# One transformer block on one core: the self-attention stage with its softmax reciprocal on GpSimd, its rotation in two products, its statistics woven and one power for two layer norms

## The reference, cut to what matters

```python
x = x + xattn(layernorm(x), ctx_1024, ...)            # cross-attention, its own layer norm behind it
x = x + attn(layernorm(x), ...)                       # self-attention: the stage that is changed
x = x + ffn(layernorm(x), ...)                        # a shared expert and 2 of 8 routed ones

def attn(x):                                          # x: 64 sequences of 64 rows, 256 columns
    q, k, v = (x @ W.T + b  per W, b), split in 16 heads of 16 columns
    q, k = rope(q), rope(k)                           # x1*cos - x2*sin ; x1*sin + x2*cos on the two halves of a head
    scores = q @ k.T * 16**-0.5
    attn = softmax(scores, axis=-1)
    return (attn @ v) @ Wo.T + bo
layernorm(x) = (x - mean) / sqrt(var + 1e-5)
```

## Time and profile before

| what | value |
| --- | --- |
| time, median of 3 runs | 2171.07 us (2169.53 to 2171.08) |
| time of the profiled execution | 2171.83 us |
| its span | 2170.1 us |
| TensorE busy, share of the span | 2109.5 us, 97% |
| VectorE busy | 1576.1 us, 73% |
| ScalarE busy | 1275.5 us, 59% |
| GpSimd busy | 951.1 us, 44% |
| softmax product of tile 0 starts (L1430) | 1409.33 us |
| softmax product of tile 31 starts | 1644.40 us |

### The profile page before, as it was taken

The page is one execution under the profiler, slowest core; times in us unless marked ns, Lnnn a source line. Parts: engine busy times, 40 slices in busy tenths (PEclk is TensorE's granted clock), DMA queues, the critical chain, the costliest instruction groups (busy, mean ns, idle before and its releaser), DMA issues.

```text
span 2170.1 us, 46318 instructions
## 1 busy us (share of the span) xinstructions
PE 2109.5 (97%) x15864; PEld 1851.0 (85%) x15865; DVE 1576.1 (73%) x2833; ACT 1275.5 (59%) x3067; POOL 951.1 (44%) x813
## 2 busy tenths in 40 slices
PE   8999999999999999999999999899998999999997
PEld 7898888898888888888888888677776888888886
DVE  7667767767767677677677676689996887666665
ACT  5566666656656665666656556477775335555553
POOL 5223322322333332233223323388885234777775
PEclk9999999999999999999999999999999999999999
DMA  4000000010010010000100100245533222333332
GB/s 154 11 21 25 22 22 24 10 34 19 14 34 19 14 34 14 19 24 13 31 24 10 34 10 1 81 140 152 152 121 100 88 78 54 54 53 53 54 55 42
DMA packets 100686, 103.91 MB, mean 48 GB/s; under 512 B 11952, under 2 KB 90160, under 8 KB 100624
## 3 DMA queue, kind: packets, MB, share of 16 engines
q1 hardware_dynamic: 86992, 84.47, 12.6%
q0 software_dynamic: 13632, 18.62, 5.3%
HBM read 72.52 MB, written 30.54 MB: 47 GB/s over the span
## 4 chain that ended last, share of the span: by engine, by line
PE 59%; DVE 17%; issue 9%; POOL 9%; ACT 3%; DMA 2%; DVEq 0%; POOLq 0%; SPq 0%; ACTq 0%
PE banks L915 33%; PE banks L958 6%; PE banks L988 5%; PE banks L1016 5%; POOL out_dram L2393 4%; PE banks L1003 3%; POOL r_x L2357 3%; DVE top L678 2%; DVE q_st L658 2%; DMA out_dram<-r_y,index 2%; PE banks L2232 2%; POOL index L2364 2%; DVE peak L675 2%; DVE s_peak L1550 1%; DVE s_rsum L1596 1%
## 5 line engine op out<-in xcount | busy, mean ns | idle before, releaser
L915 PE MATMUL banks<-ctxT_hi,qk_hi 128*128 128x256 f32 x1024 | 300.8, 294 | 0.0
L915 PE MATMUL banks<-ctxT_hi,qk_lo 128*128 128x256 f32 x1024 | 289.8, 283 | 0.0
L915 PE MATMUL banks<-ctxT_lo,qk_hi 128*128 128x256 f32 x1024 | 287.4, 281 | 0.0
L547 ACT ACTIVATE probs<-banks,nbias 128x256 f32<-128x256 f32 x512 | 236.0, 484 | 83.7 <-DVE nbias L680 83.3
L436 POOL TENSOR_TENSOR rinv<-rsum,inverse 128x4 f32<-128x4 f32 x96 | 96.7, 1008 | 408.3 <-ACT probs L547 408.3
L554 ACT ACTIVATE pc<-banks 128x512 f32<-128x512 f32 x256 | 153.0, 598 | 191.0 <-PE banks L915 187.9
L638 DVE TENSOR_TENSOR qk_lo<-banks,qk_hi 128x512 fp32r<-128x512 f32 x256 | 163.4, 685 | 88.0 <-ACT qk_hi L509 88.0
L675 DVE TENSOR_REDUCE peak<-banks 128x4 f32<-128x1024 f32 x128 | 156.3, 1221 | 90.6 <-PE banks L915 90.4
L915 PE MATMUL banks<-pT_hi,ctx_hi 128*128 128x512 f32 x512 | 205.2, 401 | 1.7 <-DVE pT_lo L638 1.7
L638 DVE TENSOR_TENSOR pT_lo<-banks,pT_hi 128x512 fp32r<-128x512 f32 x256 | 165.5, 684 | 56.7 <-ACT pT_hi L509 56.2
L915 PE MATMUL banks<-pT_hi,ctx_lo 128*128 128x512 f32 x512 | 202.3, 395 | 0.0
(11 more groups left out here) (273 smaller groups left out, 6195.1 us busy)
## 6 DMA issues: line engine op xcount, KB each, us to landing
ctx_raw<-in_ctx_dram SPq DMA_DIRECT2D x64, 256.0 KB, 2.7
experts_w<-in_L_ffn_We_dram SPq DMA_DIRECT2D x24, 512.0 KB, 4.0
x_in<-in_x_dram SPq DMA_DIRECT2D x16, 256.0 KB, 2.8
x_again<-in_x_dram SPq DMA_DIRECT2D x16, 256.0 KB, 2.8
x_stream<-z SPq DMA_DIRECT2D x16, 256.0 KB, 2.1
s_x<-x_stream SPq DMA_DIRECT2D x32, 128.0 KB, 3.8
s_x_again<-x_stream SPq DMA_DIRECT2D x32, 128.0 KB, 2.1
x_normalised<-s_xl SPq DMA_DIRECT2D x32, 128.0 KB, 1.7
```

What stands on the lines that cost most here:

```text
L547: nc.scalar.activation(probs[:, s % 2, p, :], scores[:, s % 2, p // 2, (p % 2) * SK:(p % 2 + 1) * SK], ACT.Exp, bias=nbias[:, s % 2, p:p + ...
L915: last = nc.tensor.matmul(out, a, b, start=(n == 0), stop=(n == 3 * len(pairs) - 1))
```

## The change

Four edits, all in the self-attention stage:

1. VectorE's RECIPROCAL of the 16 softmax sums is gone. GpSimd raises the sums to the power -1 (a `tensor_tensor` with 128x16 elements) right before the softmax product, with a wait on `rsum_done` ahead of it and a wait for its own result behind it.
2. The rotation's three products become two of 512 columns, over a table in another order, into one tile `spun` with two halves; GpSimd adds the halves as it did before.
3. VectorE's statistics of the two layer norms stand together: two `bn_stats`, two `bn_aggr`, and one addition of epsilon on two columns. They stand ahead of the rotation; before, those of tile n-2 stood behind it.
4. GpSimd takes both inverse roots with one power on two columns at the head of the step; the second `rstd` power ahead of `xl` is gone.

```diff
-LINKS_PER_PAIR = 16
+LINKS_PER_PAIR = 12
...
-    table = np.concatenate([cos, cos, -sin, sin], axis=1)
+    table = np.concatenate([cos, sin, -sin, cos], axis=1)
...
-                sp.wait_ge(l3_stats, g.tile(s, -1))
+                sp.wait_ge(ln_stats, g.tile(s, 4))
...
-    def rotate(src, out_cos, out_sin, done):
+    def rotate(src, w):
...
-        done[0](nc.vector.tensor_tensor(heads(out_cos), heads(src), angles(0, HD), ALU.mult))
-        done[1](nc.vector.tensor_tensor(heads(out_sin)[:, :, 0:h], heads(src)[:, :, h:HD], angles(HD, h), ALU.mult))
-        done[2](nc.vector.tensor_tensor(heads(out_sin)[:, :, h:HD], heads(src)[:, :, 0:h], angles(HD + h, h), ALU.mult))
+        return nc.vector.tensor_tensor(
+            spun[:, w, :].rearrange("p (h e d) -> p h e d", e=2, d=h),
+            src.rearrange("p (h w d) -> p w h d", w=2, d=h)[:, w].unsqueeze(2).broadcast_to([P, 2 * SH, 2, h]),
+            table[:, w * HD:(w + 1) * HD].rearrange("p (e d) -> p e d", d=h).unsqueeze(1).broadcast_to([P, 2 * SH, 2, h]),
+            ALU.mult)
...
-    def normalised(pool, out, src, which, ready, done, nth):
-        pool.wait_ge(ready, nth)
-        nc.gpsimd.tensor_tensor(rstd[:, which:which + 1], mv[:, which, 1:2], power[:, :],
-                                ALU.pow).then_inc(done, 1)
-        pool.wait_ge(done, nth)
-        pool.sem_inc(pool_past, 1)
+    def inverse_spread(pool, g, s):
+        first, second = g.has(s, 3), g.has(s, -2)
+        if first or second:
+            pool.wait_ge(ln_stats, g.tile(s, 4))
+            which = slice(0 if first else 1, 2 if second else 1)
+            nc.gpsimd.tensor_tensor(rstd[:, which], mv[:, which, 1], power[:, which], ALU.pow).then_inc(rstd_done, 1)
+            pool.wait_ge(rstd_done, g.tile(s, 4))
+            pool.sem_inc(pool_past, 1)
...
     def pool_step_at(pool, g, s):
+        inverse_spread(pool, g, s)
...
-            nc.gpsimd.tensor_tensor(turned[:, :], turned[:, :], swapped[:, :], ALU.add).then_inc(turn_done, 1)
+            nc.gpsimd.tensor_tensor(turned, turned, spun[:, 1, :], ALU.add).then_inc(turn_done, 1)
...
         if g.has(s, 0):
+            pool.wait_ge(rsum_done, g.tile(s, 1))
+            nc.gpsimd.tensor_tensor(rinv[:, :], rsum[:, :], inverse[:, :], ALU.pow).then_inc(rinv_done, 1)
             pool.wait_ge(rinv_done, g.tile(s, 1))
...
-            ln_of(dve, x1[:, o, :], 0, ln_stats)
+            stats_1 = stats_of(x1[:, o, :], 0)
+        if g.has(s, -2):
+            wait_freed(dve, g, ("y", s))
+            stats_2 = stats_of(x2[:, s, :], 1)
+        if g.has(s, 3):
+            means = mean_of(dve, 0, stats_1)
+        if g.has(s, -2):
+            if g.has(s, -3):
+
+                dve.wait_ge(l3_done, g.tile(s, -2))
+            means = mean_of(dve, 1, stats_2)
+        if g.has(s, 3) or g.has(s, -2):
+            dve.wait_ge(dve_step, means)
+            which = slice(0 if g.has(s, 3) else 1, 2 if g.has(s, -2) else 1)
+            nc.vector.tensor_scalar(mv[:, which, 1], mv[:, which, 1], EPS, None, ALU.add).then_inc(ln_stats, 1)
...
-            link(nc.vector.tensor_reduce(rsum[:, :], probs[:, s, :].rearrange("p (h k) -> p h k", k=SQ),
-                                         AX_X, ALU.add))
-            nc.vector.reciprocal(rinv[:, :], rsum[:, :]).then_inc(rinv_done, 1)
+            nc.vector.tensor_reduce(rsum[:, :], probs[:, s, :].rearrange("p (h k) -> p h k", k=SQ),
+                                    AX_X, ALU.add).then_inc(rsum_done, 1)
```

More of the change, by code:

```diff
@@ L1219, in self_attention @@
     bvp = sb("bvp", [P, DC])
-    power = sb("power", [P, 1])
+    inverse = sb("inverse", [P, SH])
+    power = sb("power", [P, 2])
     x1 = sb("x1", [P, 2, D])
@@ L1228, in self_attention @@
     xT_lo = sb("xT_lo", [P, 2, DC, P], F32R)
-    turned = sb("turned", [P, 2 * D])
-    swapped = sb("swapped", [P, 2 * D])
+    spun = sb("spun", [P, 2, 2 * D])
+    turned = spun[:, 0, :]
     qT = sb("qT", [P, DC, P])
@@ L1255, in self_attention @@
     ln_stats = sem("ln_stats")
-    ln_rstd = sem("ln_rstd")
+    rstd_done = sem("rstd_done")
     ln_done = sem("ln_done")
-    l3_stats = sem("l3_stats")
-    l3_rstd = sem("l3_rstd")
     l3_done = sem("l3_done")
@@ L1396, in pool_start, with normalised @@
         nc.gpsimd.memset(share[:, :], 2.0 / P).then_inc(pool_setup, 1)
+        nc.gpsimd.memset(inverse[:, :], -1.0).then_inc(pool_setup, 1)
         nc.gpsimd.memset(vbd[:, :, :, :, :, :], 0.0).then_inc(pool_setup, 1)
-        pool.wait_ge(pool_setup, 3)
-    def normalised(pool, out, src, which, ready, done, nth):
-        pool.wait_ge(ready, nth)
-        nc.gpsimd.tensor_tensor(rstd[:, which:which + 1], mv[:, which, 1:2], power[:, :],
-                                ALU.pow).then_inc(done, 1)
-        pool.wait_ge(done, nth)
-        pool.sem_inc(pool_past, 1)
+        pool.wait_ge(pool_setup, 4)
+    def inverse_spread(pool, g, s):
[6 more added lines that the diff above has]
+            pool.sem_inc(pool_past, 1)
+    def normalised(out, src, which):
         return nc.gpsimd.tensor_scalar(out, src, mv[:, which, 0:1], rstd[:, which:which + 1],
@@ L1414, in pool_step_at @@
             o = (s + 1) % 2
-            normalised(pool, xn[:, :], x1[:, o, :], 0, ln_stats, ln_rstd, g.tile(s, 4)).then_inc(ln_done, 1)
+            pool.sem_inc(pool_past, 1)
+            normalised(xn[:, :], x1[:, o, :], 0).then_inc(ln_done, 1)
         if g.has(s, 2):
             wait_freed(pool, g, ("qk", s))
-            nc.gpsimd.tensor_tensor(turned[:, :], turned[:, :], swapped[:, :], ALU.add).then_inc(turn_done, 1)
+            nc.gpsimd.tensor_tensor(turned, turned, spun[:, 1, :], ALU.add).then_inc(turn_done, 1)
         if g.has(s, -2):
@@ L1425, in pool_step_at @@
                 wait_filled(pool, g, key, pairs_on)
-            normalised(pool, xl[:, s, :], x2[:, s, :], 1, l3_stats, l3_rstd, g.tile(s, -1)).then_inc(l3_done, 1)
+            pool.sem_inc(pool_past, 1)
+            normalised(xl[:, s, :], x2[:, s, :], 1).then_inc(l3_done, 1)
         if g.has(s, 0):
+            pool.wait_ge(rsum_done, g.tile(s, 1))
+            nc.gpsimd.tensor_tensor(rinv[:, :], rsum[:, :], inverse[:, :], ALU.pow).then_inc(rinv_done, 1)
             pool.wait_ge(rinv_done, g.tile(s, 1))
@@ L1537, in dve_start, with stats_of, mean_of @@
         dve.wait_ge(bias_done, 1)
-    def ln_of(dve, src, which, ready):
-        link(nc.vector.bn_stats(stats[:, which, :], src))
+    def stats_of(src, which):
+        step(nc.vector.bn_stats(stats[:, which, :], src))
+        return chain[0] + chain[1]
+    def mean_of(dve, which, stats_at):
+        dve.wait_ge(dve_step, stats_at)
         dve.sem_inc(dve_past, 1)
-        link(nc.vector.bn_aggr(mv[:, which, :], stats[:, which, :]))
-        nc.vector.tensor_scalar(mv[:, which, 1:2], mv[:, which, 1:2], EPS, None, ALU.add).then_inc(ready, 1)
+        step(nc.vector.bn_aggr(mv[:, which, :], stats[:, which, :]))
+        return chain[0] + chain[1]
     def dve_step_at(dve, g, s):
@@ L1583, in dve_step_at @@
                 dve.wait_ge(turn_done, g.tile(s, 2))
[L1584 to L1587, removed]
-                dve.wait_ge(l3_done, g.tile(s, -2))
-            ln_of(dve, x2[:, s, :], 1, l3_stats)
+            step(rotate(bank, 0))
+            rotate(bank, 1).then_inc(free, 1)
         if g.has(s, 0):
@@ L1661, in pe_step @@
             for c in range(4):
-                last = nc.tensor.transpose(bank[:, c * P:(c + 1) * P], turned[:, c * P:(c + 1) * P], ident[:, :])
+                last = nc.tensor.transpose(bank[:, c * P:(c + 1) * P], spun[:, 0, c * P:(c + 1) * P], ident[:, :])
             last.then_inc(done, 1)
```

9 lines of the change are left out of this document (3 added, 6 removed).

## The result

The changed kernel takes 2233.28 us (median of 4 runs, 2232.52 to 2234.50), the kernel before 2171.07 us (median of 4, 2169.53 to 2173.85): a ratio of 1.0282 with a 95% interval of 1.0270 to 1.0295, 62 us slower. The prediction was 2225 us with a range of 2214 to 2244. The profiled execution took 2233.07 us, its span is 2230.9 us.

What follows compares the result with a forecast made beforehand. GpSimd was to become the bound at 9.45 us a step instead of 7.74. Middle +44.5, ramp +4.2 and tail +4.5 made +53.2 us on the profiled 2171.83: 2225 us, range 2214 to 2244.

Steps and rivals of the forecast that it cites:

- The power of 16 columns: GpSimd's new reciprocal: 2.82 us on a straight line through one, two and four columns, 3.03 us added with its gap.
- the steeper: Rival: the 16-column power costs 4.03 us, in proportion to four columns, giving 2264 us; chance 0.07.
- the flat: Rival: the power costs the same for 4 as for 16 columns, giving 2170 us, no change; chance 0.03.
- the cheap rival: Rival: the 16-column power costs 0.216 us like a plain product, TensorE becomes the bound, 2163 us; chance 0.04.
- One power for both norms: On GpSimd, two one-column powers with gaps, 1.54 us, become one two-column power, 0.91 us with its gap; 0.63 us saved.
- the sum for the middle: Tiles 2 to 28: 26 GpSimd steps of 9.45 us, 245.7 us where there were 201.2, +44.5 us.
- what comes behind the last product "stays": Tail behind the softmax product of tile 31: holds neither sums nor reciprocals, so its time was to stay unchanged.
- its first rival: Rival: gaps in every middle step lower TensorE's clock; at half the time lower, +14 us, 2239 us; chance 0.08.
- Which engine stands behind: Before the change, VectorE sets the step of 7.74 us and TensorE stands right behind at about 7.3 to 7.5 us.
- VectorE's savings land in a wait: In the middle, VectorE gains a wait of 2 to 3 us a step ahead of the sums or the maximum.
- The statistics: On VectorE, statistics waits get covered and one addition goes; with the reciprocal, 0.4 to 0.8 us off its step.
- TensorE's wait at L1714 and its loop: TensorE waits for GpSimd's softmax product 1.5 to 2.2 us a step; no loop but GpSimd's own is binding.

Runs made afterwards that it cites:

- no_inc: The changed kernel without one semaphore increment in GpSimd's queue behind the wait for the power of the two variances: 2231.40 us, ratio 1.0273.
- dve_recip: The changed kernel with the reciprocal of the softmax sums back on VectorE, the other three edits kept: 2169.64 us, ratio 0.9991 to the kernel before.
- fill: The changed kernel with 12 extra identity transposes on TensorE ahead of its wait for the softmax product in each of the 24 looped steps: 2233.98 us.
- pow8: The changed kernel with GpSimd's reciprocal power on 8 of the 16 columns, the other reciprocals a constant: 2194.82 us, ratio 1.0102 to the kernel before.
- pow8_split: The changed kernel with the reciprocal power on 8 columns and epsilon added in two one-column instructions instead of one of two columns: 2190.71 us.

## Why the prediction was right, point by point

The mechanism was the one forecast: GpSimd's own row sets the step, and its new power makes it. The profiled execution took 2233.07 us where 2225.0 was the sum, 8 us more. By the rows these are 4.2 in the middle, 2.0 behind the last product, 1.0 in the ramp, and about 1 in the next stage and around the span.

**The power of 16 columns: right.** Three rows on a line gave 2.82 us; it takes 2.923. With its gap (0.07, taken as 0.21) the term is 2.99 us where 3.03 stood: it was near by luck in part, since an error of 0.10 and one of 0.14 the other way cancel. The 2.923 us lie between both bounds, 1.01 and 4.03, and refute the steeper, the flat and the cheap rival; 1.661 us at 8 columns refutes a price by blocks.

**One power for both norms: the size of one term was off.** The power itself is 0.696 us (0.698 was read). The gap behind it is 0.31 to 0.38 us and not 0.21, because more stands in the queue between the power and its reader: 0.16 us a step, of which no_inc shows 0.08 and the rest is argued. This is most of what the sum for the middle lacked: 9.61 less 9.45 is 0.16, 4.2 us in 26 steps. The rest is small and goes both ways: the rotation's sum to `xl` 1.26 and not 1.23, the product to the power 1.86 to 2.01 and not 1.90. By the latter the products stand 9.55 to 9.73 us apart, where 9.4 to 9.5 without alternation was forecast.

**The step of the sum that failed: what comes behind the last product "stays".** It grew by 2.0 us, because the tail's TensorE now waits for GpSimd (2.46 us ahead of the L1714 of the last tile but one) and then runs at the lower clock, 0.50, up to the next stage; at 1.00 the stretch takes 11.06 us. The prediction had this mechanism as its first rival, but for the middle, where it costs nothing, and not for the tail, where each product and transpose is on the path. The ramp grew by 5.2 us where 4.2 stood; that 1 us is less than what executions differ by ahead of the stage.

**Which engine stands behind: right in name, wrong in size.** TensorE was said to stand at 7.3 to 7.5 us a step. It stands at 7.6. The 0.47 us that the earlier trace rows show at L1667 are idle time of weight loads, and 8.9 of their 12.2 us are still there in dve_recip, where TensorE is the bound. The real room was 0.15 us. It did not touch the forecast, since GpSimd's loop is far above both; but it made the expectation for dve_recip wrong, 2163 instead of 2169.6. The price of the cheap-power rival is too low by that.

**VectorE's savings land in a wait: right.** 2.6 us a step where 2 to 3 were forecast. The forecast had it ahead of the sums or of the maximum; two thirds of it stand ahead of `xT_lo` instead. The rotation in two products measures 1.27 to 1.29 us together, 0.67 to 0.69 each with an overlap: no gain and no loss against three, as taken.

**The statistics: counted as a gain, and partly a cost.** One addition less is right for VectorE. That the new form can be held by GpSimd for up to 1.67 us was not foreseen. It costs up to 0.15 us in the steps where it is on GpSimd's path, 8 of 26.

**TensorE's wait at L1714 and its loop: right in kind, the wait smaller.** 1.24 us a step by the matmuls' idle time where 1.5 to 2.2 were forecast. TensorE is busy 19.1 us longer in the middle than before, 0.73 us a step; with that the wait would be 1.97 us, so the lower clock ate the difference. Its wait for VectorE at L1684, which was L1667, is gone. The granted clock of the middle fell without a longer step, and fill shows that it cost nothing there.

## What to carry to other kernels

Before work is moved to an engine that is busy 86% of a stage, take its own idle time in one step (here 0.68 us) and set it against the price of the new instruction at its real size; a power on GpSimd is priced by its columns, 0.16 us each, and an instruction of a quarter of the size in the same trace is enough to see it. Where TensorE's room is asked for, its idle time in the trace shows too much: the weight loads at L1667 showed 0.47 us a step, the matmuls 0.25, and the room was 0.15. A few extra transposes in a step measure it directly.

An edit that only saves beside the bound is worth no more than the distance to the next engine: edits 2 to 4 took 9.3 us of work and 4.8 us of waiting for its own statistics from VectorE in 26 steps, over half a microsecond a step, and the kernel got 0.15 us.

## What the runs showed of the hardware that was not expected

- A VectorE `tensor_scalar` on 128x2 elements, from and to on-chip memory, that starts during GpSimd's 128x1024 product does not end until the product has ended: 1.47 us in place of 0.17 (pow8). On 128x1 it is not held, 0.15 us as ever (pow8_split).
- One semaphore increment in GpSimd's queue between a result and its reader costs nearly 0.1 us (gap of 0.38 us against 0.29). Behind the 16-column power, where only a wait stands, the gap is 0.07 us.
- TensorE's mean granted clock in the middle fell from 1.00 to 0.92 when a gap of 1 to 2 us came into each step, and was 0.99 with the gap filled; the length of the step did not follow it. That of the stretch behind the last product did: 14.07 us at 0.50, 11.06 at 1.00.
